# A decoder's last sublayers, tile by tile, in slots between the pairs of a context attention

## The reference

```
x = x + attention(norm(x))            # 16 heads of 128, ALiBi, softmax over the 56 tokens of a sequence
x = x + context_attention(norm(x))    # q from x; k, v from ctx; 16 heads of 16; scores clipped at 50; its own norm
x = x + ternary_ffn(norm(x))          # 8-bit activations, ternary weights, silu(gate) * up, Hadamard of 1,024, down
x = x + attention_1(norm(x))          # 16 heads of 16, 4 key heads; attends over the 8 sequences, causal in them
x = x + norm(norm(x) + summary(ctx))  # the summary: a decaying weighted sum of each context sequence, projected
x = x + ffn_1(norm(x))                # 1,024 wide, rounded to steps of 0.1, gelu
```

## Time and profile before

| | us |
|---|---|
| median of 3 runs (range) | 623.88 (622.65 to 624.21) |
| the profiled execution | 621.71 |
| its span in the trace | 618.8 |
| heads and setup, to the first exponential of the context attention | 195.0 |
| context attention, 48 pairs | 235.6 |
| tail | 188.2 |

### The profile page before, as it was taken

How to read it: one execution, slowest core, us unless ns; L and a number is a source line. 1 busy time by engine, 2 the same in 40 slices (tenths; PEclk the granted TensorE clock), 3 DMA queues, 4 the chain that set the end, 5 groups by cost and what they waited for, 6 DMA issues and landing times.

```text
span 618.8 us, 15547 instructions
## 1 busy us (share of the span) xinstructions
PE 503.2 (81%) x6802; PEld 407.1 (66%) x6802; DVE 360.7 (58%) x630; ACT 211.1 (34%) x336; POOL 186.4 (30%) x83
## 2 busy tenths in 40 slices
PE   3994979999977999999999999998516766164296
PEld 2673767778765888888888888887413665143164
DVE  2236453443334686868777776764477843783652
ACT  1451323433335444444444444443102351101111
POOL 1004999500014435353525344420000001460100
PEclk9996989999989999999999999999758777656599
DMA  8720212221510111212121212100000000000001
GB/s 290 286 68 2 68 34 68 68 59 44 177 45 6 63 39 67 63 42 67 40 69 37 69 35 69 48 24 4 0 0 0 1 2 0 0 1 0 0 0 30
DMA packets 10685, 30.70 MB, mean 50 GB/s; under 512 B 1282, under 2 KB 4355, under 8 KB 9859
## 3 DMA queue, kind: packets, MB, share of 16 engines
q1 hardware_dynamic: 10434, 29.32, 14.6%
q0 software_dynamic: 192, 0.51, 0.3%
HBM read 29.36 MB, written 0.46 MB: 48 GB/s over the span
## 4 chain that ended last, share of the span: by engine, by line
PE 72%; DVE 18%; ACT 3%; issue 3%; POOL 2%; DMA 1%; DVEq 0%
PE psk L889 11%; PE psv L898 10%; PE psa L923 8%; PE psv L941 7%; PE psa L818 7%; PE psa L826 5%; PE psv L833 5%; PE psk L862 2%; PE psa L1088 2%; PE psk L1099 2%; PE psa L842 2%; DVE stats L487 2%; DVE xn L504 1%; DVE shared L541 1%; PE psk L853 1%
## 5 line engine op out<-in xcount | busy, mean ns | idle before, releaser
L630 DVE TENSOR_SCALAR shared<-shared,top 125x896 f32<-125x896 f32 x48 | 79.2, 1690 | 55.5 <-ACT shared L410 55.5
L276 POOL TENSOR_TENSOR cx<-ring,ones 128x1000 fp32r<-128x1000 f32 x24 | 45.0, 1876 | 119.1 <-DMA ring<-ctx_t_dram 119.1
L889 PE MATMUL psk<-cx,wkv 128*128 128x500 f32 x288 | 77.8, 406 | 0.0
L898 PEld LDWEIGHTS psv<-wkv,cx 128*125 128x125 f32 x552 | 71.1, 186 | 5.4 <-DVE vmem L594 2.0
L898 PE MATMUL psv<-wkv,cx 128*125 128x256 f32 x552 | 72.9, 281 | 0.6 <-DVE vmem L594 0.6
L410 ACT ACTIVATE shared<-psa 125x1792 f32<-125x1792 f32 x24 | 40.1, 1670 | 65.8 <-PE psa L923 65.8
L279 POOL TENSOR_TENSOR cx<-ring,cx 128x1000 fp32r<-128x1000 f32 x24 | 61.2, 2552 | 1.9
L410 ACT ACTIVATE smem<-psa 125x1792 f32<-125x1792 f32 x24 | 40.1, 1670 | 63.1 <-PE psa L923 63.1
L889 PEld LDWEIGHTS psk<-cx,wkv 128*128 128x128 f32 x288 | 50.5, 188 | 12.5
L923 PE MATMUL psa<-qb,kx 32*125 32x112 f32 x1536 | 54.7, 279 | 1.6 <-issue 1.6
L818 PE MATMUL psa<-xnT,whd 128*128 128x448 f32 x128 | 53.2, 561 | 0.0
(11 more groups left out here) (200 smaller groups left out, 824.7 us busy)
## 6 DMA issues: line engine op xcount, KB each, us to landing
ring<-ctx_t_dram SPq DMA_DIRECT2D x24, 500.0 KB, 3.4
whd<-heads_dram SPq DMA_DIRECT2D x16, 385.0 KB, 3.4
whd<-heads_dram SPq DMA_DIRECT2D x16, 129.0 KB, 2.2
wraw<-w_dram SPq DMA_DIRECT2D x2, 1024.0 KB, 6.0
mats_sb<-mats_dram SPq DMA_DIRECT2D x1, 1536.0 KB, 16.0
wraw<-gate_dram SPq DMA_DIRECT2D x1, 1024.0 KB, 10.1
wraw<-up_dram SPq DMA_DIRECT2D x1, 1024.0 KB, 12.2
wraw<-down_dram SPq DMA_DIRECT2D x1, 1024.0 KB, 13.9
```

Of the source, the lines that this page charges most:

```text
L276: nc.gpsimd.tensor_tensor(cx[HI][slot][:, :, :], ctxs[cs], ones[:, 0:1].unsqueeze(1).to_broadcast([P, DC, UT]), ALU.mult).then_inc(s_ch, 1)
L630: nc.vector.tensor_scalar(half, half, top[:, u // UPB, key:key + 1], 1.0 / ECLIP, ALU.min, ALU.max).then_inc(s_clip, 1)
L889: last = nc.tensor.matmul(PS[2][:, m, 0:UT], wkv[a][:, 0, c, m * P:(m + 1) * P], cx[b][u % 2][:, c, :], start=(a == b and c == 0), stop=(a ...
L898: last = nc.tensor.matmul(bank[0:CT, t * D:(t + 1) * D], cx[b][u % 2][:, c, a0:a0 + CT], wkv[a][:, 1, c, :], start=(a == b and c == 0), st ...
```

## The change

The tail is no longer behind the pairs. It is cut into steps for one tile of 112 tokens, and the steps stand in 73 *slots* (`SLOTS`): slot `s` holds pair `s` as long as there is one (`s < 48`), and steps of the tail. A tile `a` takes its first half (division to the ternary feed-forward) in 12 slots, `i` = 0 to 11, and its second half (second attention to the end) in the next 12. So slots 0 to 11 hold no tail, 12 to 23 the first half of tile 0, 24 to 35 that of tile 1 and the second half of tile 0, 36 to 47 tile 2 and 1, 48 to 59 tile 3 and 2 without pairs, 60 to 72 the second half of tile 3. Each engine has its `tail_early(s)` and `tail_late(s)` at two places of its slot. Steps by slot `i`:

| i | first half of a tile | second half of the tile before |
|---|---|---|
| 0 | `take_raw`, `turn_context` | `normalise4`, `turn_x4`, move of `tw`, `project_hidden` and `last_add` of the tile before it |
| 1 | `divide`, turn, move | `project_qkv`, moves, `score`, `project_in` |
| 2 | `project_o`, `centre_delta`, root 2 | `project_out`, softmax, `attend`, move of `sysb` |
| 3 | `add_delta`, root 3, `quantise` | turn, `project_attended` |
| 4 | `turn_xq`, move, `gate_up` (gate) | `add_proj`, root 5, `add_summary`, root 6 |
| 5 | table load, silu, table load | `add_normalised`, root 7 |
| 6 | `gate_up` (up), `times_up` | `normalise7` |
| 7 | three butterflies | turn, move, `hidden` first half, move |
| 8 | `turn_inter`, move, `hadamard` | `clip_hidden` |
| 9 | `scale_hidden`, move, `quantise_hidden` | |
| 10 | turn and move of `xq2` | `hidden` second half, move, `clip_hidden` |
| 11 | `down_proj`, `add_down`, root 4 | table load, gelu, table load |

With it: the high parts of units 2 to 23 are rounded by ScalarE (`round_up`) and no longer by GpSimd, which keeps the subtraction; ScalarE instead of VectorE moves the values out; keys and values share one PSUM bank, so that each projection waits for the other's move; VectorE weighs behind its clips and not ahead of them; the second attention is VectorE's alone; roots are Ln and Exp on ScalarE with one step of refinement on VectorE, so that the exponential's table stays loaded; the loops of the heads are unrolled, `wscale` is computed ahead of the other constants, and those move behind heads 3 to 6.

```diff
@@ SyncE
-            with sp.Fori(0, B * UPB // 3 - 1) as i:
-                for k in range(3):
-                    sp.wait_ge(s_wb, 6 * i + 2 * k + 2)
-                    sp.dma_start(ctxs[k], ctx_t[bass.ds(3 * i + 3 + k, 1)].rearrange("o p c t -> (o p) c t")).then_inc(s_ctx[k], 16)
+            for u in range(3, B * UPB):
+                sp.wait_ge(s_wb, 2 * (u - 3) + 2)
+                sp.dma_start(ctxs[u % 3], ctx_t[u]).then_inc(s_ctx[u % 3], 16)
...
@@ GpSimd
-            def split(u, slot, cs, loads):
-
-                pool.wait_ge(s_ctx[cs], loads)
-                if u >= 2:
-                    pool.wait_ge(s_vp, 2 * u - 2)
-                nc.gpsimd.tensor_tensor(cx[HI][slot][:, :, :], ctxs[cs], ones[:, 0:1].unsqueeze(1).to_broadcast([P, DC, UT]),
-                                        ALU.mult).then_inc(s_ch, 1)
-                pool.wait_ge(s_ch, u + 1)
-                nc.gpsimd.tensor_tensor(cx[LO][slot][:, :, :], ctxs[cs], cx[HI][slot][:, :, :].bitcast(F32), ALU.subtract).then_inc(s_cx, 1)
+            def split(u):
+
+                slot = u % 2
+                pool.wait_ge(s_ctx[u % 3], 16 * (u // 3) + 16)
+                if u < 2:
+                    nc.gpsimd.tensor_tensor(cx[HI][slot][:, :, :], ctxs[u % 3], ones[:, 0:1].unsqueeze(1).to_broadcast([P, DC, UT]),
+                                            ALU.mult).then_inc(s_ch, 1)
+                pool.wait_ge(s_ch, u + 1)
+                nc.gpsimd.tensor_tensor(cx[LO][slot][:, :, :], ctxs[u % 3], cx[HI][slot][:, :, :].bitcast(F32), ALU.subtract).then_inc(s_cx, 1)
...
@@ ScalarE
-            for pp in range(2 * B * UPB):
-                u, r = pp // 2, pp % 2
-                act.wait_ge(s_qk, pp + 1)
-                if pp >= 2:
-                    act.wait_ge(s_pv, pp - 1)
-                nc.scalar.activation(ex[pp % 2], psa[0:CT, :, 0:448], ACT.Exp, scale=0.25).then_inc(s_ex, 1)
-                if u + 1 < B * UPB:
-                    move_k(u + 1, r)
+            def round_up(u):
+
+                act.wait_ge(s_ctx[u % 3], 16 * (u // 3) + 16)
+                act.wait_ge(s_vp, 2 * u - 2)
+                act.wait_ge(s_kp, 2 * u - 2)
+                act.wait_ge(s_cx, u - 1)
+                nc.scalar.activation(cx[HI][u % 2][:, :, :], ctxs[u % 3], ACT.Copy).then_inc(s_ch, 1)
+
+            round_up(2)
+            for s in range(SLOTS):
+                u, r = s // 2, s % 2
+                if s < PAIRS:
+                    act.wait_ge(s_qk, s + 1)
+                    if s >= 2:
+                        act.wait_ge(s_pv, s - 1)
+                    nc.scalar.activation(ex[s % 2], psa[0:CT, :, 0:448], ACT.Exp, scale=0.25).then_inc(s_ex, 1)
+                    if u + 1 < B * UPB:
+                        move_vu(u + 1, r, kvb)
+                tail_early(s)
+                if u + 1 < B * UPB:
+                    move_k(u + 1, r, kvb)
+                tail_late(s)
+                if r == 1 and u + 3 < B * UPB:
+                    round_up(u + 3)
...
@@ VectorE
-            for pp in range(2 * B * UPB):
-                u, r = pp // 2, pp % 2
-                weigh(u, r)
-                dve.wait_ge(s_ex, pp + 1)
-                for t in range(2):
-                    key = TPU * (u % UPB) + 2 * r + t
-                    half = ex[pp % 2][:, :, t * 224:(t + 1) * 224]
-                    nc.vector.tensor_scalar(half, half, top[:, u // UPB, key:key + 1], 1.0 / ECLIP, ALU.min, ALU.max).then_inc(s_clip, 1)
-                if u + 1 < B * UPB:
-                    move_vu(u + 1, r)
-                if pp % (2 * UPB) == 0 and pp:
-                    take_raw(u // UPB - 1)
-                if pp % (2 * UPB) == 2 * UPB - 1:
-                    keep_weighted(u // UPB)
+            for s in range(SLOTS):
+                tail_early(s)
+                if s < PAIRS:
+                    clip(s)
+                    weigh(s // 2, s % 2)
+                if s % 6 == 0 and 0 < s <= PAIRS:
+                    take_raw(s // 6 - 1)
+                if s % 6 == 5 and s < PAIRS:
+                    keep_weighted(s // 6)
+                tail_late(s)
...
@@ TensorE
-            for pp in range(2 * B * UPB):
-                u, r = pp // 2, pp % 2
-                scores(pp)
-                if u + 1 < B * UPB:
-                    project_k(u + 1, r)
-                    pe.wait_ge(s_vue, 2 * u + 2 + r)
-                    project_vu(u + 1, r, PS[3][:, 0, :])
-                if pp:
-                    weighted_values(pp - 1)
+            for s in range(SLOTS):
+                u, r = s // 2, s % 2
+                if s < PAIRS:
+                    scores(s)
+                    if u + 1 < B * UPB:
+                        pe.wait_ge(s_ke, s + 2)
+                        project_vu(u + 1, r, kvb)
+                if 0 < s <= PAIRS:
+                    weighted_values(s - 1)
+                tail_early(s)
+                if u + 1 < B * UPB:
+                    pe.wait_ge(s_vue, s + 3)
+                    project_k(u + 1, r, kvb)
+                tail_late(s)
+
```

1241 lines of the change are left out of this document (690 added, 551 removed).

## The result

The changed kernel takes **673.05 us** (median of 4 runs, 672.8 to 673.79) against 623.9: a ratio of 1.079, with a 95% interval of 1.0775 to 1.0812. It is slower, as forecast, but by 49 us where 19 were forecast, and outside the range of 620 to 668. The span of the profiled execution is 670.6 us.

The account below looks back on a forecast made before the run. The context-attention pairs were taken as bound by TensorE, the rest as a chain from engine to engine. Heads 189.5 + pairs 342.7 + tail behind 106 = 638.5 us span, 643 us on the median; range 620 to 668.

Parts of the forecast that it names:

- Heads: Time up to the first exponential of the pairs: 189.5 us instead of 195.0, bounds −10 and +1.
- Tail behind the pairs: The 25 slots left after the last pair, chains of small steps: 56.5 + 49 = 106 us.
- The largest term: In the pairs, ScalarE waits for a late load: two slots take 13.2 us instead of 9.9, +70 us over 21.
- the tail work inside the slots: Tail steps exceeding free time in slots with pairs: 7.8, 11.7, then 13.4 us per round of 12 slots.
- The first rival: In the pairs, the load is not waited for: 607 us with no wait at all; chance of ending below 622, 9%.
- That the clock falls in the stage: Second rival: TensorE's clock drops during the pairs, +20 us, 663 us; chance 20%.
- That the wait hides all tail work: Third rival: in the pairs the tail work costs nothing extra, −33, 610 us; chance 3%.
- The rule beside it: VectorE and GpSimd lock a shared port pair; rounding on ScalarE halves possible lockout, only even clips meet GpSimd's subtraction.
- The three terms: Span forecast: heads 189.5, stage of the pairs 342.7, part behind the pairs 106 us.

Follow-up runs that it names:

- experiment 6: Changed kernel with the four small constant steps ahead of GpSimd's start and scan, sum and other constants behind heads 10 to 12: 652.8 us, ratio 1.048.
- experiment 12: Kernel before, with only its constants placed as in the changed kernel: 643.6 us, ratio 1.031.
- Experiment 8: Changed kernel with eight extra bfloat16 matmuls a slot on TensorE behind the last pair, into a bank nobody reads: 667.5 us, ratio 1.071.
- experiment 9: Changed kernel with the constants as in experiment 6 and VectorE's weighing at the very start of a slot: 621.3 us, ratio 0.994.
- 11: Kernel of experiment 9 plus TensorE's filling matmuls behind the last pair: 614.0 us, ratio 0.985.
- experiment 7: Changed kernel with silu and gelu replaced by plain copies, so without table loads behind the heads: 672.9 us, ratio 1.078.
- 3: Changed kernel with VectorE weighing ahead of the clips of its pair: 645.7 us, ratio 1.039.
- 4: Changed kernel with the rounding of the high parts back on GpSimd for all units: 664.4 us, ratio 1.066.
- 5: Changed kernel with ScalarE's rounding of a unit one slot later, at the end of the even slot: 646.1 us, ratio 1.039.

## Why the prediction was right and wrong

**The step that failed is "Heads"**: "189.5; bounds −10 (no cost of the moved pieces) and +1". It gave the moved pieces the durations that they had where they stood, and looked for the danger in the longest of them, the scan, "behind GpSimd's long instructions". The scan came through by its place. The shortest pieces did not: four steps of 0.2 us each became 21.2 us in a row beside GpSimd, and `binS` 1.24 instead of 0.23. (`pn` was held up too, 3.68 and 2.28 us instead of 0.62, but it is no part of the loss: the kernel before has it at 1.40, 4.77 and 1.95.) The first exponential came at 215.8, 26.3 us late; 22.2 of them go when the pieces stand elsewhere (experiment 6), and the same placement alone costs the kernel before 21.7 (experiment 12). What makes this a failed step and not bad luck is that the prediction itself had the rows: two clips beside GpSimd's subtraction took 3.35 us instead of 1.28. It applied them to the slots and not to the heads, where GpSimd's instructions are up to three times as long, and where the kernel before shows a `pn` of 4.77 us. The gain it saw was there: TensorE's wait for `wscale` fell from 7.72 to 0.64 us.

**Mis-sized: "Tail behind the pairs", 106 for 119.** The sum took a clock between the levels, by the 0.73 of the old tail; granted was 0.60. It has no term for table loads, where there are five on the chain (1.28 us each), and took `attend` from rows of plain products; its two sums, over sequences and so strided, take 2.74 and 3.60 us, where `score`'s contiguous sums of the same size take 1.75 and 2.29. The chain of waits behind the pairs has them one after the other (start, length, line):

```profile
572.04 2.74 DVE xn L822
...
584.85 1.28 ACT L396
...
587.28 1.28 ACT L401
...
611.96 1.28 ACT L459
...
614.22 1.28 ACT L401
...
635.83 3.60 DVE xn L822
...
660.22 1.28 ACT L459
```

Experiment 8 gives 5.7 us, net of the filling's own cost, to the clock, and the same filling gives 7.3 between experiments 9 and 11. The two sums are 2.3 us over. The table loads stand on the chain, but experiment 7 shows no gain that is clear of the 4.9 us by which this part varies with nothing changed in it. So some 8 of the 13 are accounted for, and where the other 5 come from stays open.

**Right: the load.** The largest term, two slots in 13.2 us instead of 9.9, was measured at 13.1; slots 0 to 11 took 295.2 − 215.8 = 79.4 us, forecast 79.4 (79.1 to 81.8 in the profiles that share this code, so that the last digit is luck). ScalarE waited for the load 16 times and not 21, for 2.25 us in the mean. Three ways of taking the wait away (3, 4, 5) each bring two slots to 11.2 to 11.4.

**Right, a little high: the tail work inside the slots.** Slots 12 to 23 took 84.2 us (forecast 87.2), 24 to 35 took 88.6 (forecast 91.1); the stage 335.8 for 342.7. The first rival had priced what the removal of the wait would give: 46 us, of which the tail work takes about 10 back. Experiment 3 gave 25, and experiment 9, with no wait left, 30; so the tail work takes back 16 and more.

**The rivals.** That the load is hidden anyway: no, 36 us of waiting. That the clock falls in the stage: hardly, 0.98. But it does fall here and there where two slots take 13.1 us, and not in slots without tail at 11.2. These are windows of the changed kernel, a pair of slots and then one that follows it:

```profile
254.00:267.00 13.00, 10.34 (x229) 8.56 (x229) 4.64 (x9) 6.62 (x8) 2.30 (x1) 1.00 0.15 42
267.00:274.00 7.00, 5.24 (x105) 3.98 (x104) 2.53 (x4) 3.65 (x4) 2.29 (x1) 0.76 0.01 2
```

TensorE had waited 1.76 us for the move of the values; then its six key matmuls took 2.83 us instead of 1.63, and this even half 6.48 instead of 4.95. In the kernels with 11.2 us for two slots the even halves without tail all agree within 0.03 us but for the first. That the wait hides all tail work: no.

**The rule beside it** held in its direction. In the changed kernel only the even clips meet GpSimd's subtraction, and take 0.96 us each, the odd ones 0.68; with the rounding on GpSimd again the even ones take 1.61.

The three terms add up to 638.2 (the prediction wrote 638.5, a slip of 0.3), and +26.3 (heads), −6.9 (stage) and +13.0 (behind it) lead to the span of 670.6.

## What to carry to other kernels

Before a small VectorE step is moved, look what GpSimd runs at its new place: beside an instruction of 7 us a cast or `tensor_scalar` of three columns costs up to 7 us. An earlier place costs 0.2. The same arithmetic as `scalar_tensor_tensor` costs 0.2 in the last part of GpSimd's instruction, and what is left of its first 4.4 us otherwise. When a load is released late in a loop, put its first reader a stage later or its last reader first; both were worth 27 us here, and neither moves any work to another engine. When the removal of a wait gives less than the wait was long, look for what had lain under it.
